# A selective-scan layer's work ahead of its scan: half-width projections, other places for a convolution, a dt group and three copies

## The reference, cut to what matters

```
xz = einsum('bld,ed->ble', xn, in_proj_w)       # 256 -> 1024
x_inner, z = split(xz, 2)                       # 512 channels each
xc = silu(causal depthwise conv(x_inner, 4 taps) + conv_b)
x_ssm = einsum('bld,ed->ble', xc, x_proj_w)     # 33 rows: B (16), C (16), dt (1)
dt = softplus(x_ssm[..., -1:] * dt_w[:, 0] + dt_b)
A = -exp(A_log)                                 # 512 x 16
h = exp(dt * A) * h + (dt * u) * B_t            # u = xc, 128 steps, state 16
y_t = sum(h * C_t, axis=-1) + D_param * u_t
y = y * silu(z);  out = einsum('ble,de->bld', y, out_proj_w) + residual
```

## Time and profile before

| | us |
|---|---|
| median of 3 runs | 853.94 |
| lowest and highest run | 852.97, 859.43 |
| the profiled execution's own time | 856.85 |
| its span, first to last instruction | 854.6 |
| TensorE, VectorE, ScalarE, GpSimd busy | 694.7, 673.3, 529.8, 497.3 |

### The profile page before, as it was taken

The page is one execution under the profiler, slowest core; times in us unless marked ns, Lnnn a source line. Parts: engine busy times, 40 slices in busy tenths (PEclk is TensorE's granted clock), DMA queues, the critical chain, the costliest instruction groups (busy, mean ns, idle before and its releaser), DMA issues. The chain is left out here.

```text
span 854.6 us, 22547 instructions
## 1 busy us (share of the span) xinstructions
PE 694.7 (81%) x8285; PEld 522.1 (61%) x8285; DVE 673.3 (79%) x1498; ACT 529.8 (62%) x1439; POOL 497.3 (58%) x528
## 2 busy tenths in 40 slices
PE   4899999999999989369999708988889988851464
PEld 3578888888888776158899503345555555441333
DVE  6767778898888976667788557789889998679867
ACT  2644555566555655236676595579899787019296
POOL 2057777777777875045555176118899898424211
PEclk9999999999999999669999858999999999975778
DMA  7827000000000410027775533032333332010001
GB/s 295 279 94 301 1 2 2 7 1 8 1 8 8 161 51 14 7 69 217 225 201 147 120 115 89 2 100 78 102 101 127 103 108 96 3 49 0 1 13 38
DMA packets 30347, 71.44 MB, mean 84 GB/s; under 512 B 5472, under 2 KB 19488, under 8 KB 28320
## 3 DMA queue, kind: packets, MB, share of 16 engines
q1 hardware_dynamic: 25680, 57.54, 19.3%
q0 software_dynamic: 4560, 12.46, 6.1%
HBM read 59.57 MB, written 10.42 MB: 82 GB/s over the span
## 5 line engine op out<-in xcount | busy, mean ns | idle before, releaser
L1911 POOL TENSOR_TENSOR arena<-arena 128x1024 f32<-128x1024 f32 x63 | 147.2, 2385 | 29.1 <-DVE arena L1850 23.5
L1850 DVE TENSOR_TENSOR_SCAN arena<-arena,ps 128x1024 f32<-128x1024 f32 x64 | 141.8, 2270 | 14.1 <-ACT arena L1720 6.9
L1537 PEld LDWEIGHTS ps<-arena 64*64 64x64 f32 x4096 | 79.6, 134 | 63.9 <-DVE arena L1850 25.5
L1537 PE MATMUL ps<-arena 64*64 64x64 f32 x4096 | 92.0, 223 | 17.9 <-issue 8.9
L647 PE MATMUL ps<-arena 128*128 128x128 f32 (+1 forms) x768 | 101.2, 282 | 0.9 <-PEq L376 0.9
L647 PEld LDWEIGHTS ps<-arena 128*128 128x128 f32 (+1 forms) x768 | 91.7, 193 | 14.1 <-issue 12.9
L852 ACT ACTIVATE arena<-arena 128x128 f32<-128x128 f32 x256 | 98.8, 390 | 1.2 <-DVE arena L776 1.1
L1088 POOL DMA_INDIRECT arena<-tokens,arena x63 | 60.8, 965 | 59.6 <-PE ps L1124 42.4
L860 ACT ACTIVATE arena<-ps 128x512 f32<-128x512 f32 x64 | 38.2, 597 | 86.6 <-PE ps L666 86.6
L907 POOL TENSOR_TENSOR arena<-arena 128x512 f32<-128x512 f32 x64 | 66.7, 1043 | 21.5 <-DVE arena L782 21.5
L897 POOL TENSOR_TENSOR arena<-arena 128x256 f32<-128x256 f32 x64 | 47.9, 748 | 46.2 <-DVE arena L762 46.2
(11 more groups left out here) (326 smaller groups left out, 1522.1 us busy)
## 6 DMA issues: line engine op xcount, KB each, us to landing
arena<-c_rows SPq DMA_DIRECT2D x32, 512.0 KB, 3.7
arena<-in_E_gu SPq DMA_DIRECT2D x8, 1024.0 KB, 12.9
expert_out<-arena SPq DMA_DIRECT2D x63, 128.0 KB
arena<-in_E_dn SPq DMA_DIRECT2D x1, 4096.0 KB, 13.3
arena<-in_ctxT SPq DMA_DIRECT2D x2, 1024.0 KB, 5.1
arena<-in_A_o SPq DMA_DIRECT2D x1, 2048.0 KB, 16.6
arena<-in_X_o SPq DMA_DIRECT2D x1, 2048.0 KB, 23.7
arena<-in_F_w SPq DMA_DIRECT2D x4, 512.0 KB, 5.2
```

The lines of the kernel that those rows point to most:

```text
L1537: t = eng.matmul(psD[d][cols, k, at:at + R], dtuT[rows, b, c, cols], diagB[rows, i % 2, b, :], start=True, stop=True)
L1850: eng.tensor_tensor_scan(hst[s % 4], dA[s % 4], psD[s % 2].rearrange("p k m -> p (k m)"), 0.0, ALU.mult, ALU.add).then_inc(h_ready, 1)
L1911: eng.tensor_tensor(hC[s % 4], hst[s % 4], Csb[i % 4], ALU.mult).then_inc(hC_ready, 1)
```

## The change

Seven edits in the stretch ahead of the scan and in its first slots; the amount of arithmetic is the same.

1. `bc_dt`: each matmul of 512 columns becomes two of 256 columns (`quarter`), the second writing to partitions 64 to 96. `bc_rows` becomes two copies.
2. VectorE: the third convolution of half 0 stands ahead of the last `combine`.
3. Half 0's silu order is 0, 1, 3, 2 and all four, `bc_dt(0)`, `bc_rows(0)` and `dt_rows(0)` stand ahead of the projections of half 1.
4. Half 1's projections and copies come in the order 0, 3, 1, 2 (`XI_ORDER`).
5. ScalarE: `bc_rows(1)` stands ahead of the exponential of negA.
6. Gate copies: VectorE 4, ScalarE 2; ScalarE's first decay stands behind its first transposed copy; `turn_dtu(2)` stands behind `dBu(1)`, `turn_dtu(3)` behind `dBu(3)`; on ScalarE `scaled(2)` stands ahead of `turned_dtu(3)`.
7. VectorE: `dt_and_dtu(3)` stands behind the first scan. The first two C loads go to yg and no longer wait for the gate rows.

```diff
-        Z_FIRST, Z_MOVED, Z_COPIED = 2, 3, 3
+        Z_FIRST, Z_MOVED, Z_COPIED = 2, 4, 2
-        XC_ORDER = ((0, 3, 1, 2), (0, 1, 2, 3))
+        XC_ORDER = ((0, 1, 3, 2), (0, 1, 2, 3))
+        XI_ORDER = ((0, 1, 2, 3), (0, 3, 1, 2))
+        def quarter(v, n):
+            return v[:, n * 2 * P:(n + 1) * 2 * P]
-        Csb = [view(33792, 1024), view(34816, 1024), yg[:, 2], yg[:, 3]]
+        Csb = [yg[:, 2], yg[:, 3], view(33792, 1024), view(34816, 1024)]
...
-                eng.wait_ge(z_done, 2 * CT)
                 for i in range(2 * ST):
+                    if i == 2:
+                        eng.wait_ge(z_done, 2 * CT)
...
-                            t = eng.matmul(ps[0:E + 1, PROJ_BANK[k], :], w_bc[:, c, :], half(xc[:, c], k),
-                                           start=n == 0, stop=n == CT - 1)
+                            for q in range(2):
+                                t = eng.matmul(ps[q * R:q * R + E + 1, PROJ_BANK[k], 0:2 * P], w_bc[:, c, :],
+                                               quarter(xc[:, c], 2 * k + q), start=n == 0, stop=n == CT - 1)
...
-                bc_dt(0, 0, CT - 1)
+                bc_dt(0)
                 eng.wait_ge(z_ready, Z_FIRST)
                 normS.pe(eng, tiles=HALVES[1])
+                dt_rows(0)
                 eng.wait_ge(normS.hT_ready, 4)
-                for m in range(CT):
+                for m in XI_ORDER[1]:
                     project(m, XI_BANK[1][m], 1).then_inc(xi_done, 1)
-                bc_dt(0, CT - 1, CT)
-                dt_rows(0)
...
                 turn_dtu(0)
-                eng.wait_ge(z_copied, 2)
+                eng.wait_ge(z_moved, Z_MOVED)
+                eng.wait_ge(z_copied, 1)
                 turn_dtu(1)
-                eng.wait_ge(z_moved, Z_MOVED)
                 dBu(0)
-                turn_dtu(2)
                 eng.wait_ge(z_copied, Z_COPIED)
                 dBu(1)
-                turn_dtu(3)
+                turn_dtu(2)
                 for s in range(SLOTS + 2):
                     if 0 < s < SLOTS - 1:
                         dBu(s + 1)
+                    if s == 2:
+                        turn_dtu(3)
...
                 conv(1, 0)
+                conv(2, 0)
                 combine(HB + 3)
...
-                conv(2, 0)
...
-                for c in range(CT):
+                for c in range(CT - 1):
                     dt_and_dtu(c)
                 eng.wait_ge(c_stored, 32)
                 for s in range(SLOTS):
                     scan(s)
+                    if s == 0:
+                        dt_and_dtu(CT - 1)
```

More of the change, by code:

```diff
@@ L1734, in _ @@
                 turned_dtu(0)
-                for n in range(Z_FIRST + Z_MOVED + 1, 2 * CT):
-                    gate_copy(n)
+                decay(0)
+                gate_copy(Z_FIRST + Z_MOVED + 1)
                 turned_dtu(1)
-                decay(0)
                 decay(1)
```

21 lines of the change are left out of this document (11 added, 10 removed).

## The result

| | before | changed |
|---|---|---|
| median of 20 runs each, us | 855.75 | 858.9 |
| lowest and highest run | 851.62, 861.77 | 854.94, 863.39 |
| profiled execution, and its span | 856.85, 854.6 | 857.99, 856.2 |

The ratio of the times is 1.0043, with a 95% interval of 1.0025 to 1.0062: the change costs 3.7 us (2.1 to 5.3; the two medians lie 3.2 us apart). The forecast was +1.5 us and 855.4 us. Part of the distance is the base, whose median over 20 runs is 1.8 us above that of the three runs shown before; the rest is the change's own.

What follows compares the result with a forecast made beforehand. GpSimd's products were taken to set the pace from the fifth, at 589.29. It would come 0.7 us earlier, the collision adds 2.2: +1.5 us on 853.94 gives 855.4 us, range 851.3 to 858.8.

Steps and rivals of the forecast that it cites:

- the chain to scan 3: Scan 1, B u of slot 3, group 3's transposes, copy and decay put scan 3 at 582.8 before the collision.
- the overlap: Half-width B, C, dt matmuls on TensorE run side by side: 1.8 us for half 1 instead of 3.6.
- the collision: Fourth dt group's two-operand VectorE operations and GpSimd's first product block each other; scan 1 starts 2.2 us later.
- The front: Work ahead of the scan: early convolution costs 1.0 us, B, C, dt copies and second dt steps come about 2 us earlier.
- The order on TensorE: Group 3's transposes stand behind B u of slot 3, which waits for scan 1; 4.3 of the 4.6 us are given back.
- T: Start of scan 0 on VectorE, forecast at 571.3, 4.6 us earlier than before.
- The forecast's own step from scan 3: Adds 2.29 + 1.43 + 1.90 us to scan 3: fifth product at 588.5, 0.7 us earlier than 589.29, before the collision.
- Rival 1: VectorE beside GpSimd's first product: no collision or half of it, 853.2 to 854.3 us; chance 0.2.
- rival 2: B, C, dt halves on TensorE don't overlap: +1.8 us, 857.2 us with the collision; chance 0.1.
- rival 4: The 4.6 us at scan 0 arrive whole and scan 3 isn't held: 849.3 us; chance 0.05.
- Rival 3: Behind the row of eight products, gaps of up to 2 us come or go: 853.5 or 857.5 us; chance 0.15.
- the two signs of being wrong: Fifth product starts before 588.3, or starts near 590.8 and the end doesn't follow it.

Runs made afterwards that it cites:

- kernel 8: Changed kernel with only the work up to the logarithms changed, and B, C, dt again in matmuls of 512 columns with one copy each: ratio to before 0.9998.
- 10: Kernel before with only B, C, dt split into two matmuls of 256 columns and two copies: ratio to before 0.9992.
- 11: Kernel before with B, C, dt in half-width matmuls and the copy of half 1 ahead of the exponential of negA: ratio to before 0.9986.
- Kernel 1: Changed kernel with one wait added: GpSimd's first product waits until the fourth dt group is done. Ratio to before 0.9993.
- Kernel 2: Changed kernel with 24 useless transposes on TensorE between B u of slots 2 and 3, filling its wait: ratio to before 1.0016.
- kernel 6: Changed kernel with all four dt groups ahead of the scan, transposes of group 3 left behind B u of slot 3: ratio to before 0.9973.
- 4: Tail only: kernel before with edits 6 and 7, without the places of the C loads. Ratio to before 1.0045.
- kernel 5: Changed kernel with the transposes of group 3 ahead of B u of slot 3 instead of behind it: ratio to before 1.0008.
- kernel 9: Changed kernel with all four dt groups ahead of the scan and the transposes of group 3 ahead of B u of slot 3: ratio to before 0.9952.
- kernel 7: Changed kernel with GpSimd's first product waiting for the fourth dt group and the transposes of group 3 ahead of B u of slot 3: ratio to before 0.9979.
- kernel 3: Front only: changed kernel with edits 1 to 5, gate copies, transposes, decays and dt groups as before. Ratio to before 0.9966.

## Why the forecast was right or wrong

**The step that failed.** In the chain to scan 3 the forecast priced B u of slot 3 and the transposes behind it from rows at TensorE's full clock, and gave no cost to the wait that the change itself puts ahead of them. The order, the overlap and the collision were as forecast. The working is below.

**The front, right.** The projections started 1.0 us later (forecast 1.0). The fourth group's convolution ended at 550.98; counted as in the profile before, 551.59 (forecast 551.6). The halves ran side by side, 1.92 us (1.8). The copies were done at 553.65, or 554.26 (554.15). The first dt group came 1.85 us earlier (1.9 to 2.0). What the forecast didn't say, and kernels 8, 10 and 11 show: of the five edits the halves carry this, and need the earlier copy. The Trainium skill (TensorEngine Tiling (Array Packing), "Key Properties") states that different tiles of the array run in parallel; the 0.12 us per record agrees, with different moving data in the two halves.

**The collision, right in place and price.** The first product was held to 3.25 us, the second operation took 3.26 us (forecast 3.4), scan 1 came 6.6 us behind scan 0 (6.8). Kernel 1 takes 2.04 us of it away (forecast 2.2). The Trainium skill's rule on two SBUF inputs (SBUF — State Buffer, "Who interferes with whom") holds. In the forecast's reading, GpSimd gets in between two VectorE operations that depend on each other, and the times fit it: the product, recorded from 574.88, is held until the first operation ends at 575.92 and then runs to 578.13; the second, recorded from 575.95, does its work only in the 1.1 us from there to 579.21.

**The order on TensorE, right; two of its terms, wrong in size.** "So scan 3 starts at T + 4.6 + 2.29 (scan 1) + 1.45 (B u 3) + 1.09 (transposes) + 1.02 (copy) + 1.04 (decay 3) = T + 11.5", with the collision T + 13.7. Measured: T + 15.3. The terms 1.45 and 1.09 are the ones that were mis-sized. They came from rows at the full clock, and the change itself puts a wait of 5.13 us ahead of them: they took 2.35 and 1.97 us, 1.8 together beyond the forecast. Kernel 2 takes away just that. From scan 3 on the forecast holds again (5.74 us to the fifth product, forecast 5.6 to 5.7).

**Scan 0, partly by chance.** Forecast 571.3, measured 572.51, or 573.12 counted from the transposes. Of these 1.8 us, 1.4 are the transposes and B u of slot 0 at a clock of 0.72, which happened in this profile and in that of kernel 6, but not in the second profile of the changed kernel nor in 1, 2, 4, 5, 7 and 9, which have the same code at this place. Without it the forecast was 0.4 us short. Whether such stretches belong to the change's price is open. From 16 us behind the first transposes to scan 0, six of the eleven profiles with half-width matmuls have one (changed, its second profile, 1, 6, 10 and 11), at four different places, and none of the three with full width (before, 4 and 8). That is too few to tell the halves from chance.

**The sum.** Without them the fifth product would stand at 79.08 - 1.4 = 77.7, 3.5 us later than before; the forecast had 1.5. Of the 2.0 us between, 1.8 are the clock; scan 0 adds 0.4 and the collision was 0.2 cheaper. (The forecast's own step from scan 3 comes to 588.4, not 588.5, so -0.9 rather than -0.7; this changes nothing.) The runs say 3.7, with 2.1 to 5.3 around it. That 858.9 lies only 0.1 us outside the range says little: without the 1.8 us of the base it would have been inside, by luck, with the same step wrong. That a microsecond at the fifth product arrives as one at the end holds only roughly: in the table, fifth product and ratio go together, but the runs are 0.2 to 2.6 us better than the fifth product says (tail only +5.1 and +3.9, changed with fourth transposes early +1.3 and +0.7, changed +4.9 and +3.7, kernel 9 -2.1 and -4.1, kernel 1 +2.0 and -0.6). From the fifth product to the end of the last it is 147.21 us before and 145.66 after. But the changed kernel's second profile has 143.83, and the others lie between 143.36 (tail only) and 147.70 (kernel 9), so one pair of profiles doesn't show that a loss at the start comes back there. Which of those gaps goes, and why, wasn't tried.

**The rivals.** Rival 1 (no collision) falls with the 3.26 us, rival 2 (no overlap) with the 1.92 us, rival 4 (all arrives) with scan 3. Rival 3 (the pace later changes) stays open: the stretch behind the fifth product is 1.6 us shorter in this pair of profiles, and the two profiles of the changed kernel differ by 1.8 us there. The case that came wasn't among them: that a wait made by the change slows the work behind it. The range ended at 858.8 because it allowed for one gap more, not for this. Neither of the two signs of being wrong that the prediction named covers it: the fifth product came neither before 588.3 nor near 590.8, but at 593.58 (594.2 counted from the transposes).

## What to carry to other kernels

Work that starts earlier is worth what arrives at the stage that sets the pace: here 2.5 to 4.2 us at the first scan (58.31 and 58.01 in the changed kernel and 56.64 in kernel 2, against 60.80) were less than nothing at the fifth product, since the dt group and the transposes that made the earlier start possible stood again in the chain of scans 1 and 3. When a change makes TensorE wait, price what it does next at both clock levels, from rows at either: 64 small matmuls took 1.48 us at the one and 2.35 at the other. And a VectorE operation with two SBUF operands that is moved beside a GpSimd operation can have the price of that operation added to its own (here 2.04 us), unless one of the two is told to wait.

## What the runs showed of the hardware that was not expected

- TensorE's clock fell behind waits as short as 1.81 us (kernel 1: 1.91 us for B u, 1.97 for the transposes, 0.72 in 577 to 581.4) and 1.77 us (kernel 5, 0.50 in 581.4 to 586), while behind waits of 0.5 to 1.3 us between slots it stayed at 1.00 in kernels 3, 7 and 9. It isn't as simple as the length of one wait: in kernel 6 the second transposes took 1.68 us behind a wait of 1.33, in kernel 7 1.07 behind the same, and in kernel 8 two slots of B u took 4.09 us behind 0.70, where kernel 3 had 2 x 1.48 and a wait of 0.70 between them. So short waits go with falls in some profiles and not in others, and what decides is open. The Trainium skill (TensorE: Matmul & The Clock Gate, "HAM oscillation — how this bites in real kernels") describes waits between groups of matmuls as the cause of such falls; kernel 2 agrees, where filling the wait kept the clock at 1.00; the falls in kernels 6 and 8 aren't explained by it.
- One program's low stretches don't all come at the same place: the projections of half 1 took 7.13 us in one profile of the changed kernel and 8.83 in the other, and the transposes ahead of scan 0 took 1.58 and 1.06. The stretch behind the 4 to 5 us wait came in both. Two profiles can thus differ by 1.5 us without any edit between them.
- A wait added on GpSimd made the kernel faster: 0.9993 with it, 1.0043 without, each against before.
